# Two row groups moved to other places in TensorE's hand-written order of a Mamba and retrieval layer

## The chip, the cores and the metric

The kernel runs on one core of one Trainium2 chip. The metric is the device time of one execution in microseconds (us). The time before the change is 3161.11 us, the median of 3 runs (3151.85 to 3166.98).

## The reference

4096 tokens of 512 numbers pass through a Mamba-2 block and then through a retrieval layer, each followed by a residual and a layer norm, all in float32.

```
zxbcdt = u @ W_in                         # gate z, conv input xBC, step sizes dt
xBC = silu(causal_conv(xBC)); x, B, C = split(xBC)
y = scan over chunks of 64 with states    # 16 heads of 64
y = rms_norm((y + x*D) * silu(z)) @ W_out
x1 = layernorm(u + y)
h = silu(x1 @ W_up.T + b_up) @ W_down.T + b_down      # 256 wide
scores of h @ W_q.T against two sets of 64 keys, 8 heads, top 8 of 8x8 sums
64 picked rows of an embedding of 4096 (256 + 512 numbers each) per token:
out = sum over rows k of silu(h . down[k] * softmax[k]) * up[k]
result = layernorm(x1 + out)
```

## The kernel before

The tokens are cut into 32 tiles of 128. Tile `i` is in three stages at once: while the loop body `tile(i)` runs, the Mamba block of tile `i + 1` is computed (the calls under `if ahead`), tile `i` gets its projections up and down and its key scores, and the 64 picked rows of tile `i - 1` are worked off (the calls `old(...)`); the first four row groups of tile `i` itself close the body (`new(...)`). The picked rows have numbers 0 to 63.

**The rows.** POOL gathers row k of all 128 tokens with one indirect DMA (L276) into one of 13 ring buffers, k modulo 13. The gather of row k waits until row k - 13 has been used. For a row that VectorE (DVE) adds up, that is told row by row (`row_used`). For a row that TensorE (PE) adds up, it is told by the semaphore `row_pe`, which rises once at the end of each group with PE rows. DVE forms the dot product of each row with h (`dot`, L1129); ScalarE (ACT) makes the coefficients of a group (`coefs`, L645) and, for rows of PE, a diagonal matrix of them (`diag_c`, L654, four buffers); then PE multiplies diagonal and row in two passes (`weighted`, L500), or DVE adds the row two groups later (`weigh`, L1143).

The 64 rows are cut into 22 groups. Those that matter here, with P for a row of PE and D for one of DVE: group 13 holds rows 39 to 42 (PPPD), 14 rows 43 and 44 (PP), 15 rows 45 to 47 (PDD), 16 rows 48 to 51 (PPPP), 17 row 52 (D), 18 rows 53 to 55 (DDD), 19 rows 56 to 59 (PPPD), 20 row 60 (D), 21 rows 61 to 63 (PDD). So the gathers of rows 52 to 54 wait for group 13 on PE, those of rows 56 and 57 for group 14, that of row 58 for group 15, and those of rows 61 to 63 for group 16.

**The orders.** Each engine runs a list written out by hand, `tile` of its own block, and takes nothing out of turn. PE's order around the change: the turn of h (L481), key scores (L488), the two halves of the next tile's gate projection `z_proj` (L359, 8 passes each), group 13, the four masked sums `step_sums` (L368), `turn_x` (eight transposes of x, L376, then five small products up to L384, which raises `cb_mm`), groups 14 and 15, `y_off` (L396), group 16, `y_diag` (L412 and L415), groups 18 and 19, `state_in` (L425), `turn_y` (L431), group 21, `out_proj` (L441).

ACT's order there: 12 of the 16 masked steps (L700), coefs of group 13, `conv_silu` (L685), the last masked steps, the gates (L710, one for each half of `z_proj`), coefs of 14 and 15, the decays: four exponentials (L715, each after its masked sum), three small ones (L718 to L720, after `cb_mm`), a copy (L724); then `soft_exp`, `skip_term` (L691), coefs of 16 and 17 with a load of the activation table, and the first half of `end_decay` (L732).

DVE's order there: top 8 and their indices, groups 14 to 17 with sorting work between them, the indices of tile i (L1108), `scaled_x` (L982), `masked_products` (L991), groups 18 to 21, and then `scan_out` (L1000), `scan_add`, `scan_gate` (L1013). `scan_out` stands behind the dot product of row 63, and `turn_y` of PE waits for `scan_gate`.

Of the kernel before, what the change touches and what calls it, by code (L numbers as in the profile page):

```python
# [78 lines left out]
def build(nc, uT, u, W_in, W_out, W_upT, W_downT, W_q, keysT, embed, consts, iota8, conv_w, conv_b,  # L79
          dt_bias, A_log, D_cols, norm_cols, b_up, b_down, out):  # L80
    with ExitStack() as ctx:
# [206 lines left out]
        def _(pe):  # L288
# [40 lines left out]
            def xbc_proj(i, first, part):  # L329

                if part == 0:
                    pe.wait_ge(ut_in, 16 * i + 16)
                if part == 2:
                    pe.wait_ge(xr_ok, 3 * i + 1)
                elif not first:
                    pe.wait_ge(st_ok, 2 * i - 1 + part)
                lo, hi = part * BANK, min(part * BANK + BANK, CONV)
                for k in range(KD):
                    m = pe.matmul(bank[XR_BANKS[part]][:, 0:hi - lo], uT_v[:, k, :], w_in[:, k, DI + lo:DI + hi],  # L339
                                  start=(k == 0), stop=(k == KD - 1))  # L340
                m.then_inc(xr_mm, 1)

            def turn_xbc(i, first, part):

                pe.wait_ge(xr_ok, 3 * i + part + 1)
                if not first:
                    if part == 0:
                        pe.wait_ge(y_ok, 2 * i)
                    else:
                        pe.wait_ge(yT_ok, 2 * i)  # L350
                for c in range(4 * part, min(4 * part + 4, KC)):
                    m = pe.transpose(bank[XBC_BANKS[part]][:, (c % 4) * P:(c % 4 + 1) * P], seg[:, c, :], ident)
                m.then_inc(xbc_mm, 1)

            def z_proj(i, b):
                if b == 0:
                    pe.wait_ge(tap_ok, PARTS * (i + 1))
                for k in range(KD):
                    m = pe.matmul(bank[Z_BANKS[b]][:, :], uT_v[:, k, :], w_in[:, k, b * BANK:(b + 1) * BANK],  # L359
                                  start=(k == 0), stop=(k == KD - 1))  # L360
                m.then_inc(z_mm, 1)

            def step_sums(i, b):

                if b >= 2:
                    pe.wait_ge(z_ok, 2 * i + b - 1)
                pe.wait_ge(am_ok, 4 * i + b + 1)
                pe.matmul(bank[SEG_BANKS[b]][:, :], later, seg[:, 4 * b:4 * b + 4, :],  # L368
                          start=True, stop=True).then_inc(seg_mm, 1)

            def turn_x(i):
                pe.wait_ge(xc_ok, i + 1)
                for c in range(KX):
                    if c % 4 == 0:
                        pe.wait_ge(e_ok, 4 * i + 1 + c // 4)
                    m = pe.transpose(bank[XT_BANKS[c // 4]][:, (c % 4) * P:(c % 4 + 1) * P], xc[:, c, :], ident)  # L376
                    if c % 4 == 3:
                        m.then_inc(xT_mm, 1)
                pe.wait_ge(e_ok, 4 * i + 3)
                pe.transpose(bank[MISC][:, 0:P], xc[:, KX, :], ident)  # L380
                pe.matmul(bank[MISC][:, P:2 * P], xc[:, KX, :], xc[:, KX + 1, :], start=True, stop=True)
                pe.matmul(bank[MISC][:, 2 * P:2 * P + NH], upto, cur[:, 1, :], start=True, stop=True)
                pe.matmul(bank[MISC][:, 2 * P + NH:2 * P + 2 * NH], later, cur[:, 1, :], start=True, stop=True)
                pe.matmul(bank[MISC][:, 3 * P:3 * P + NH], ones, cur[:, 1, :], start=True, stop=True)\  # L384
                    .then_inc(cb_mm, 1)
# [60 lines left out]
            def turn_x1(i):  # L446
                pe.wait_ge(x1_ok, i + 1)
                for k in range(KD):
                    m = pe.transpose(bank[X1T][:, k * P:(k + 1) * P], x1_new[:, k * P:(k + 1) * P], ident)
                m.then_inc(x1T_mm, 1)  # L450

            def up_proj(i, b, first, ahead):
                if b == 0:
                    if first:
                        pe.wait_ge(w_up_in, 16)
                    pe.wait_ge(x1T_ok, i + 1)
                if b < 2:
                    pe.wait_ge(st_ok, 2 * i + b + 1)
                elif ahead:
                    pe.wait_ge(tap_ok, PARTS * (i + 1) + b - 1)  # L460
                for c in range(4 * b, 4 * b + 4):
                    for k in range(KD):
                        m = pe.matmul(bank[UP_BANKS[b]][:, (c % 4) * P:(c % 4 + 1) * P],  # L463
                                      w_up[:, k, c * P:(c + 1) * P], x1T[:, k, :], start=(k == 0), stop=(k == KD - 1))
                m.then_inc(h1_mm, 1)

            def down_proj(i, b, first, ahead):
                if b == 0:
                    if first:
                        pe.wait_ge(w_down_in, 16)  # L470
                pe.wait_ge(h1_ok, 4 * i + b + 1)
                for c in range(4 * b, 4 * b + 4):
                    m = pe.matmul(bank[DOWN][:, 0:DP], h1T[:, c, :], w_down[:, c, :],  # L473
                                  start=(c == 0), stop=(c == KU - 1))
                if b == 3:
                    m.then_inc(hp_mm, 1)
# [15 lines left out]
            def weighted(t, g, first):  # L492


                for k in rows_of(g, "P"):
                    n = PE_ROWS.index(k)
                    pe.wait_ge(diag_ok, len(PE_ROWS) * t + n + 1)
                    if n == 0 and not first:
                        pe.wait_ge(sum_ok, 3 * t - 2)
                    m = pe.matmul(bank[SUM][:, :], diag_c[:, (len(PE_ROWS) * t + n) % DIAGS, :], ring[:, k % RING, DP:ROW],  # L500
                                  start=(n == 0), stop=(n == len(PE_ROWS) - 1))
                if rows_of(g, "P"):
                    m.then_inc(row_pe, 1)

            def tile(i, first, ahead):

                def old(*which):
                    for g in which:
                        if not first:
                            weighted(i - 1, g, False)  # L510

                def new(*which):
                    for g in which:
                        weighted(i, g, first)

                if ahead:
                    xbc_proj(i + 1, False, 0)
                    xbc_proj(i + 1, False, 1)
                    xbc_proj(i + 1, False, 2)
                    turn_xbc(i + 1, False, 0)  # L520
                    turn_xbc(i + 1, False, 1)
                    turn_xbc(i + 1, False, 2)
                turn_x1(i)
                old(4, 5, 6)
                up_proj(i, 0, first, ahead)
                up_proj(i, 1, first, ahead)
                up_proj(i, 2, first, ahead)
                old(7, 8)
                up_proj(i, 3, first, ahead)
                down_proj(i, 0, first, ahead)  # L530
                old(9)
                down_proj(i, 1, first, ahead)
                old(10)
                down_proj(i, 2, first, ahead)
                down_proj(i, 3, first, ahead)
                turn_h(i, ahead)
                old(11, 12)
                key_scores(i, 0)
                key_scores(i, 1)
                if ahead:  # L540
                    z_proj(i + 1, 0)
                    z_proj(i + 1, 1)
                old(13)
                if ahead:
                    step_sums(i + 1, 0)
                    step_sums(i + 1, 1)
                    step_sums(i + 1, 2)
                    step_sums(i + 1, 3)
                    turn_x(i + 1)
                old(14, 15)  # L550
                if ahead:
                    y_off(i + 1, False)
                old(16, 17)
                if ahead:
                    y_diag(i + 1, False, 0)
                    y_diag(i + 1, False, 1)
                old(18, 19)
                if ahead:
                    state_in(i + 1)
                    turn_y(i + 1)  # L560
                old(20, 21)
                if ahead:
                    out_proj(i + 1, False, 0)
                new(0)
                if ahead:
                    out_proj(i + 1, False, 1)
                new(1, 2, 3)
# [777 lines left out]
```

## Time and profile before

| | |
|---|---|
| median of 3 runs | 3161.11 us |
| profiled execution | 3151.04 us, span 3149.2 us |
| granted TensorE clock, mean | 0.953 of full |
| PE busy | 2790.8 us, 89% |
| DVE busy | 2777.5 us, 88% |
| ACT busy | 2049.7 us, 65% |
| POOL busy | 2062.7 us, 65% |
| HBM read | 845.38 MB, mean 271 GB/s over the span |

All times are of one profiled execution, counted from its first instruction. A tile takes some 93 us. No engine is busy all the time; which one holds up the others has to be read from the waits. In a timeline a row gives start, duration, engine, line and operation, and in brackets the idle time ahead of it with what ended it.

### The profile page before, as it was taken

What the parts mean: (1) busy time and instruction counts of PE and PEld (TensorE: products, weight loads), DVE (VectorE), ACT (ScalarE), POOL (GpSimd) and SP (SyncE); (2) the same over time, 40 slices, a digit from 0 to 9 for tenths busy, and PEclk for the clock granted to TensorE, in tenths of its full rate; (3) what the DMA queues carried; (4) which work ended last, traced back from release to release, by engine and by line L of the source; (5) the groups of instructions that cost most, each with busy time, mean ns of one, the idle gap of its engine ahead of it and who ended that gap; (6) DMA issues with size and microseconds to landing.
All of it is one profiled execution on the core that took longest, in us unless ns stands there. A gap on an engine that the chain in (4) does not pass through costs nothing.

```text
span 3149.2 us, 44785 instructions
## 1 busy us (share of the span) xinstructions
PE 2790.8 (89%) x11776; PEld 1737.3 (55%) x11776; DVE 2777.5 (88%) x10160; ACT 2049.7 (65%) x6513; POOL 2062.7 (65%) x2056
## 2 busy tenths in 40 slices
PE   7989899998898999999899989899898999898863
PEld 4565456655555655555566545556555565555541
DVE  3489899998899999999899989999999999899986
ACT  3466766666776666676666676666676666677642
POOL 0066666676676667666667666666766666766676
PEclk9999999999999999999999999999999999999986
DMA  8088888888888888888888888888888888888888
GB/s 284 23 263 275 270 279 273 277 290 282 272 285 265 270 292 287 276 282 277 265 277 297 273 276 271 273 278 290 284 277 268 276 272 288 283 278 281 277 303 272
DMA packets 189855, 856.76 MB, mean 272 GB/s; under 512 B 36192, under 2 KB 39392, under 8 KB 189088
## 3 DMA queue, kind: packets, MB, share of 16 engines
q0 software_dynamic: 163840, 805.44, 77.0%
q1 hardware_dynamic: 19104, 34.87, 3.2%
q10 hardware_dynamic: 6656, 13.60, 1.2%
q8 instruction: 93, 1.52, 0.2%
q14 instruction: 162, 1.33, 0.1%
HBM read 845.38 MB, written 8.39 MB: 271 GB/s over the span
## 4 chain that ended last, share of the span: by engine, by line
PE 38%; DVE 32%; DMA 9%; POOL 9%; issue 7%; ACT 5%; POOLq 0%; SPq 0%; DVEq 0%; ACTq 0%
DVE bank L1143 14%; POOL ring L276 9%; DMA ring<-embed,idx 9%; PE bank L500 8%; DVE ring L1129 8%; PE bank L359 7%; DVE xc L974 6%; PE bank L339 5%; PE bank L441 4%; PE bank L488 4%; PE bank L368 3%; ACT xc L679 1%; PE bank L376 1%; PE bank L307 1%; ACT xskip L691 1%
## 5 line engine op out<-in xcount | busy, mean ns | idle before, releaser
L276 POOL DMA_INDIRECT ring<-embed,idx x2048 | 2061.4, 1007 | 1074.8 <-issue 532.3
L1143 DVE SCALAR_TENSOR_TENSOR bank<-ring,coef,bank 128x512 f32<-128x512 f32 x1312 | 992.4, 756 | 7.4 <-issue 0.2
L1129 DVE SCALAR_TENSOR_TENSOR ring<-ring,hcur 128x256 f32<-128x256 f32 x2048 | 823.8, 423 | 138.5 <-DMA ring<-embed,idx 136.1
L645 ACT ACTIVATE coef<-prob,zp 128x1 f32<-128x1 f32 x2048 | 456.0, 286 | 630.8 <-DVE ring L1129 625.4
L500 PE MATMUL bank<-ring,diag_c 128*128 128x512 f32 x1344 | 672.8, 631 | 115.9 <-ACT diag_c L654 101.3
L463 PE MATMUL bank<-zs,w_up 128*128 128x128 f32 x4096 | 502.2, 287 | 69.2 <-ACT zs L767 65.8
L463 PEld LDWEIGHTS bank<-zs,w_up 128*128 128x128 f32 x4096 | 496.2, 203 | 110.2 <-ACT zs L767 91.8
L500 PEld LDWEIGHTS bank<-ring,diag_c 128*128 128x128 f32 x1344 | 247.2, 199 | 379.2 <-issue 223.7
L974 DVE SCALAR_TENSOR_TENSOR xc<-raw,taps,xc 128x128 f32<-128x128 f32 x960 | 266.2, 351 | 102.6 <-ACT xc L679 102.5
L339 PE MATMUL bank<-w_in,ut 128*128 128x512 f32 (+1 forms) x768 | 285.8, 524 | 4.0 <-ACT seg L667 3.9
L654 ACT ACTIVATE diag_c<-cst,coef 128x128 f32<-128x128 f32 x672 | 234.8, 394 | 48.4 <-PE bank L500 38.0
L441 PE MATMUL bank<-w_out,xdec 128*128 128x512 f32 x512 | 245.5, 635 | 0.9 <-ACT xdec L749 0.9
L359 PE MATMUL bank<-w_in,ut 128*128 128x512 f32 x512 | 228.1, 599 | 4.4 <-ACT xc L679 4.4
L339 PEld LDWEIGHTS bank<-w_in,ut 128*128 128x128 f32 x768 | 143.9, 190 | 153.1 <-issue 124.6
L473 PE MATMUL bank<-w_down,seg 128*128 128x256 f32 x1024 | 226.3, 379 | 0.0
L773 ACT ACTIVATE seg<-bank,bup 128x128 f32<-128x128 f32 x512 | 145.4, 365 | 124.1 <-PE bank L463 124.1
L473 PEld LDWEIGHTS bank<-w_down,seg 128*128 128x128 f32 x1024 | 192.1, 190 | 24.8
L441 PEld LDWEIGHTS bank<-w_out,xdec 128*128 128x128 f32 x512 | 107.7, 212 | 149.8 <-issue 127.8
L1129 DVE DVE_READ_ACCUMULATOR ring<-ring,hcur 128x1 f32 x2048 | 177.0, 86 | 0.0
L359 PEld LDWEIGHTS bank<-w_in,ut 128*128 128x128 f32 x512 | 98.3, 192 | 128.5 <-issue 128.5
L700 ACT ACTIVATE seg<-cst,cur 128x128 f32<-128x128 f32 x512 | 155.6, 391 | 0.0
L415 PEld LDWEIGHTS bank<-xdt,seg 128*128 128x128 f32 x1024 | 133.6, 196 | 8.7 <-issue 8.7
(144 smaller groups left out, 3422.2 us busy)
## 6 DMA issues: line engine op xcount, KB each, us to landing
ring<-embed,idx POOLq DMA_INDIRECT x2048, 4.6
ring<-uT SPq DMA_DIRECT2D x4, 2048.0 KB, 14.2
ut<-uT SPq DMA_DIRECT2D x32, 256.0 KB, 6.5
zs<-u SPq DMA_DIRECT2D x32, 256.0 KB, 5.6
out<-acc SPq DMA_DIRECT2D x32, 256.0 KB, 4.6
w_up<-W_upT ACTq DMA_DIRECT2D x1, 4096.0 KB, 13.0
w_in<-W_in ACTq DMA_DIRECT2D x1, 2560.0 KB, 17.4
w_in<-W_in ACTq DMA_DIRECT2D x1, 2048.0 KB, 22.0
```

Of the source, the lines that this page charges most:

```text
L276: pool.indirect_dma_start(out=ring[:, k % RING, :], out_offset=None, in_=embed, in_offset=bass.IndirectOffsetOnAxis(ap=idx[:, half, k:k + ...
L339: m = pe.matmul(bank[XR_BANKS[part]][:, 0:hi - lo], uT_v[:, k, :], w_in[:, k, DI + lo:DI + hi], start=(k == 0), stop=(k == KD - 1))
L359: m = pe.matmul(bank[Z_BANKS[b]][:, :], uT_v[:, k, :], w_in[:, k, b * BANK:(b + 1) * BANK], start=(k == 0), stop=(k == KD - 1))
L441: m = pe.matmul(bank[OP][:, :], yT[:, c * P:(c + 1) * P], w_out[:, c, :], start=(c == 0), stop=(c == KX - 1))
L463: m = pe.matmul(bank[UP_BANKS[b]][:, (c % 4) * P:(c % 4 + 1) * P], w_up[:, k, c * P:(c + 1) * P], x1T[:, k, :], start=(k == 0), stop=(k == ...
L473: m = pe.matmul(bank[DOWN][:, 0:DP], h1T[:, c, :], w_down[:, c, :], start=(c == 0), stop=(c == KU - 1))
L500: m = pe.matmul(bank[SUM][:, :], diag_c[:, (len(PE_ROWS) * t + n) % DIAGS, :], ring[:, k % RING, DP:ROW], start=(n == 0), stop=(n == len(P ...
L645: m = act.activation(coef[:, k:k + 1], prob_v[:, k:k + 1], ACT.Silu, scale=zp[:, k:k + 1])
L654: act.activation(diag_c[:, (len(PE_ROWS) * t + n) % DIAGS, :], ident, ACT.Copy, scale=coef[:, k:k + 1]).then_inc(diag_ok, 1)
L974: m = dve.scalar_tensor_tensor(out=xc[:, c, :], in0=raw[:, c, j:j + P], scalar=taps[:, c, j:j + 1], in1=xc[:, c, :], op0=ALU.mult, op1=ALU ...
L1129: m = dve.scalar_tensor_tensor(out=ring[:, k % RING, 0:DP], in0=ring[:, k % RING, 0:DP], scalar=1.0, in1=hcur[:, :], op0=ALU.mult, op1=ALU ...
L1143: dve.scalar_tensor_tensor(out=total if n == len(DVE_ROWS) - 1 else running[:, :], in0=ring[:, k % RING, DP:ROW], scalar=coef[:, k:k + 1], ...
```

## The change

In PE's list, group 13 is put between the two halves of the next tile's gate projection, where it stood behind both, and group 14 between the four masked sums and `turn_x`, where it stood behind `turn_x`. Nothing else is touched: the orders of ACT, DVE and POOL and every semaphore's counts stay.

```diff
--- before.py
+++ after.py
@@ -539,15 +539,17 @@
                 key_scores(i, 1)
                 if ahead:
                     z_proj(i + 1, 0)
+                old(13)
+                if ahead:
                     z_proj(i + 1, 1)
-                old(13)
-                if ahead:
                     step_sums(i + 1, 0)
                     step_sums(i + 1, 1)
                     step_sums(i + 1, 2)
                     step_sums(i + 1, 3)
+                old(14)
+                if ahead:
                     turn_x(i + 1)
-                old(14, 15)
+                old(15)
                 if ahead:
                     y_off(i + 1, False)
                 old(16, 17)
```

## Rows read from the trace of the kernel before

**Rows 1.** Section 4 of the page: the chain that ended last, by engine.

```profile
PE 38%; DVE 32%; DMA 9%; POOL 9%; issue 7%; ACT 5%; POOLq 0%; SPq 0%; DVEq 0%; ACTq 0%
```

**Rows 2.** Waits of the whole span: total us, times, longest.

```profile
POOL ring L276 <- PE bank L500: 289.2, 151, 4.9
...
DVE ring L1129 <- DMA ring<-embed,idx: 136.1, 214, 2.5
...
ACT decay L718 <- PE bank L384: 24.0, 32, 1.2
```

**Rows 3.** Timeline of PE in tile 21, from 2100 to 2138 us.

```profile
2100.41 7.03 PE L359 MATMUL bank<-w_in,ut 128*128 128x512 f32 x16
2107.28 2.74 PE L500 MATMUL bank<-ring,diag_c 128*128 128x512 f32 x6
2109.86 3.60 PE L368 MATMUL bank<-seg,cst 128*128 128x512 f32 x8
2113.50 1.06 PE L376 MATMUL bank<-cst,xc 128*128 128x128 f32 x8
...
2115.37 2.82 PE L500 MATMUL bank<-ring,diag_c 128*128 128x512 f32 x6
...
2121.27 3.70 PE L500 MATMUL bank<-ring,diag_c 128*128 128x512 f32 x8 [1.36 <-ACT diag_c L654]
...
2136.32 1.54 PE L431 MATMUL bank<-cst,xdt 128*128 128x128 f32 x8 [2.93 <-DVE xdt L1013]
```

**Rows 4.** Timeline of ACT in the same tile.

```profile
2107.48 0.60 ACT L710 ACTIVATE zs<-bank 128x512 f32<-128x512 f32 x1 [2.71 <-PE bank L359]
...
2110.06 0.40 ACT L654 ACTIVATE diag_c<-cst,coef 128x128 f32<-128x128 f32 x1 [1.18 <-PE bank L500]
...
2115.55 0.19 ACT L718 ACTIVATE decay<-bank 128x16 f32<-128x16 f32 x1 [0.73 <-PE bank L384]
...
2120.81 1.28 ACT L654 ACTIVATE diag_c<-cst,coef 128x128 f32<-128x128 f32 x4
```

**Rows 5.** Timeline of POOL there: the gathers of rows 56, 60, 61 and 63.

```profile
2117.60 1.00 POOL L276 DMA_INDIRECT ring<-embed,idx  x1 [2.59 <-PE bank L500]
...
2122.67 2.08 POOL L276 DMA_INDIRECT ring<-embed,idx  x1 [0.30 <-issue]
2125.24 0.94 POOL L276 DMA_INDIRECT ring<-embed,idx  x1 [0.50 <-PE bank L500]
...
2127.77 0.94 POOL L276 DMA_INDIRECT ring<-embed,idx  x1 [0.30 <-issue]
```

**Rows 6.** Timeline of DVE there: the dot products of rows 60 and 63.

```profile
2127.97 0.43 DVE L1129 SCALAR_TENSOR_TENSOR ring<-ring,hcur 128x256 f32<-128x256 f32 x1 [0.96 <-DMA ring<-embed,idx]
...
2132.23 0.43 DVE L1129 SCALAR_TENSOR_TENSOR ring<-ring,hcur 128x256 f32<-128x256 f32 x1 [0.24 <-DMA ring<-embed,idx]
```

**Rows 7.** All 2048 gathers (line L276): from issue to landing.

```profile
DMA to landing us min/median/max: 3.8/4.6/8.6
```

**Rows 8.** Timeline of POOL in tile 15: the gather of row 61.

```profile
1563.48 1.04 POOL L276 DMA_INDIRECT ring<-embed,idx  x1 [0.30 <-issue]
```

**Rows 9.** Windows of 3.70 us over group 16 (L500): us, PE busy, clock, DMA share, GB/s.

```profile
248.40:252.10 3.70, 3.68 (x8) 1.00 0.86 294
...
1558.80:1562.50 3.70, 3.66 (x8) 1.00 0.56 202
...
2962.00:2965.70 3.70, 3.68 (x8) 1.00 0.89 297
```

**Rows 10.** Windows of 4.00 us from the start of turn_y (L431), same columns.

```profile
263.60:267.60 4.00, 1.97 (x8) 0.50 0.81 273
...
2977.00:2981.00 4.00, 1.96 (x8) 0.64 0.93 294
```

**Rows 11.** Windows from turn_y to out_proj's end, tiles 8 and 21 (PE, PEld, DVE, ACT, POOL busy; clock).

```profile
919.70:929.10 9.40, 9.09 (x26) 4.08 (x26) 8.46 (x28) 6.92 (x21) 7.27 (x8) 1.00 0.96 341
2136.30:2146.90 10.60, 10.58 (x27) 5.38 (x28) 9.35 (x28) 7.95 (x23) 8.01 (x9) 0.84 0.96 334
```

More of the change, by code:

```diff
@@ L541, in tile @@
                     z_proj(i + 1, 0)
-                    z_proj(i + 1, 1)
                 old(13)
                 if ahead:
+                    z_proj(i + 1, 1)
                     step_sums(i + 1, 0)
```

## The prediction

> **What bounds the kernel now.** I read the chain that ended last first. No engine owns it: PE has 38% of it, DVE 32%, DMA and POOL 9% each [rows 1]. So the tiles follow one another by a relay, and only a step on the relay is worth anything. The list of waits shows two places where this change can touch it: POOL stands 289.2 us in all waiting for PE to finish row groups, and DVE waits 136.1 us for gathered rows to land [rows 2].
>
> Then I followed one tile through the timelines of four engines, tile 21. PE runs without a gap through both halves of the gate projection, group 13, the masked sums, the turn of x and groups 14 and 15 (from 2100.41 on); then it sits idle for 1.36 us ahead of group 16, because ACT hasn't made its first diagonal, and for 2.93 us ahead of the turn of y, because DVE hasn't gated y [rows 3]. ACT's diagonals for group 16 begin at 2120.81, and the last wait ahead of them is at 2115.55: 0.73 us for the end of the turn of x [rows 4]. It is there in all 32 tiles, 24.0 us in total [rows 2]. POOL waits for group 14 before row 56 (2.59 us), and for group 16 before row 61 (0.50 us) [rows 5]. DVE waits 0.96 us for row 60 and 0.24 us for row 63, the last dot product ahead of the scan's output [rows 6]. So the relay is: turn of x on PE, decays, skip term and coefficients on ACT, group 16 on PE, gathers 61 to 63, dot product of row 63, scan on DVE, turn of y on PE. The wait for row 60, which comes from group 14, is the other, parallel strand. Both are nearly level: what one gives is lost where the other is late.
>
> **The change part by part.** Nothing is added or removed; 10 passes of PE in each of 30 tiles (`ahead` and old rows present) change places.
>
> *Group 13 forward.* Its 6 passes take 2.58 us (2107.28 to 2109.86 [rows 3]). They now run ahead of the second gate half. The diagonals are there by then: ACT makes them ahead of `conv_silu`, the last masked steps and the first gate, and has all of that behind it at 2104.77, when it begins to wait for the second half (2107.48 less 2.71 [rows 4]). POOL gets rows 52 to 54 free some 3.4 us sooner (one half of 6.87 us, 2100.41 to 2107.28). The second half of the projection ends 2.58 us later, and so does the gate that waits for it (2107.48 [rows 4]). Behind that gate on ACT stand the coefficients of 14 and 15 and the exponentials. ACT's 1.18 us wait for group 13 ahead of the diagonal at 2110.06 [rows 4] is gone, so it is 2.58 - 1.18 = 1.4 us late at the exponentials. Behind them comes the 0.73 us wait for the turn of x, so this alone would cost 0.7 us; but that wait moves too.
>
> *Group 14 forward.* Its 4 passes are two thirds of the 2.65 us or so that groups 14 and 15 take: 4 x 0.43 = 1.72 us (group 13's 2.58 over 6 gives 0.43 [rows 3]). The diagonals are ready: the second is now done at about 2111.8 and PE gets there at 2113.4. Group 14 ends 2.0 us sooner (the turn of x takes 1.87 us, 2113.50 to 2115.37), and POOL's wait of 2.59 us ahead of row 56 ends by as much sooner [rows 5]. That takes away DVE's 0.96 us at row 60 [rows 6]. The price is that the turn of x, and with it the signal that ACT awaits at 2115.55, comes 1.72 us later. This is more than the 0.7 us above and contains it. ACT has no further wait up to the diagonals at 2120.81, so they come 1.72 us later, and so does group 16: its idle time goes from 1.36 to 3.08 us. PE's own order in between (group 15, `y_off`) ends where it did.
>
> *What stands behind group 16.* The gathers of rows 61 to 63. Row 61 was issued 0.27 us after group 16's end (2121.27 + 3.70 = 2124.97, 2125.24 [rows 3, 5]), so it goes to 2126.96 and row 63 from 2127.77 to 2129.5. Row 63 landed by 4.46 us after its issue (2132.23 [rows 6]). With that, its dot product is 1.72 us late; with the shortest landing of any gather, 3.8 us [rows 7], it is 1.06 us late. POOL has paused longer, so the queue is emptier; I take the middle, 1.4 us. The 0.96 us won at row 60 can't be kept, because DVE then waits for 61 to 63. Everything after, scan, turn of y, output projection, next tile, follows the dot product of row 63. PE's later `y_diag` and `state_in` are covered: PE had 2.93 us idle there, and loses 1.72.
>
> In seven of 30 tiles POOL was late on its own account at row 61: the window over group 16 moved about 200 GB/s there instead of 290 [rows 9]. In tile 15 row 61 went out at 1563.48 [rows 8], 0.98 us after group 16's window closed, so 0.7 of the 1.72 us is swallowed; and row 63 wasn't waited for. I take 0.5 us (between 0 and 1.0). Sum of the order alone: 23 x 1.4 + 7 x 0.5 = 36 us; from 23 x 1.06 = 24 to 23 x 1.72 + 7 x 1.0 = 47.
>
> *The clock.* Ahead of the turn of y, PE is idle for about 3 us (2.93 in tile 21), and in the 4 us behind it the granted clock is 0.50 to 0.68 in 28 of 30 tiles, that is, much of it at 1.2 GHz in place of 2.4 [rows 10]. Behind the 1.36 us ahead of group 16 it is 1.00 in all 30 [rows 9]. The change makes these 1.36 into 3.08 us, which is the first kind. The price of such a stretch: from the turn of y to the output projection's end, tile 21 at clock 0.84 needs 10.5 us, tile 8 at 1.00 needs 9.25 [rows 11]: 1.25 us. As lost clock it is 10.6 x 0.16 = 1.7. Below it is nothing, if group 16 escapes. I take 1.25 us in 28 of 30 tiles, 35 us. It falls on group 16, hence on the gathers, and isn't hidden. Against it, the idle time ahead of the turn of y shrinks to about 2.7 us, and there some of the slow stretches may go: I take a quarter off, 9 us.
>
> The Trainium skill (TensorE: Matmul & The Clock Gate, Part 1: The HAM clock gate) says the array goes back to half clock when it has been idle and must be busy for a time before full clock returns; that speaks against this change. By that rule group 16 would run slowly and the time come out with this term, 3223 us; without the rule's effect at this place it would be 3197 us. The trace agrees behind the turn of y [rows 10], and shows no such effect after the shorter idle time ahead of group 16 [rows 9].
>
> Sum: 36 + 35 - 9 = +62 us. The profiled execution took 3151 us (span 3149.2), 10 below the median of the runs; on the median it gives 3161 + 62 = 3223 us.
>
> **The rivals.**
>
> *Order alone* (chance 0.27): group 16 keeps the full clock. +36 us, 3197 us (3185 to 3208). For it: the idle time is only just that of the turn of y. Against: 28 of 30 tiles there.
>
> *No difference* (0.09): the slow stretch leaves the turn of y and doesn't appear at group 16. Then -1.25 meets +1.4 per tile: +4 us, 3165 us. It needs an idle time ahead of the turn of y that no longer drops the clock; tile 8 shows that it can stay at 1.00 [rows 11].
>
> *Faster* (0.09): it does what the earlier gathers promise. If group 16 isn't held by the turn of x but by something that doesn't move, DVE saves 0.96 + 0.24 us a tile [rows 6] plus what lies behind it: some 1.3 x 30 = 39 us, 3122 us. It decides at ACT's L718: if that wait is not on the path to the diagonals of group 16, the gain stays; as soon as group 16 is late by over 0.3 us, row 63 takes it back. The 0.73 us idle there in front of a busy stretch up to 2120.81 [rows 4] speaks against it.
>
> *My forecast* (0.55): order and clock, 3223 us, own range 3200 to 3258 (the upper end 47 + 30 x 1.7 = +98).
>
> **How the numbers follow.** Range 3177 to 3258: from a little below the order term's lower bound to both terms at their upper ones; it leaves out the two last rivals. A difference below 0.5%, 16 us, can't be told from none in this kernel. Slower 0.82, same 0.09, faster 0.09.
>
> **What the profile after would show.** POOL's waits ahead of rows 52 and 56 shrink by 2 to 3 us each; the wait ahead of row 61 grows from 0.5 to 5 us or more. PE's idle time ahead of group 16 is about 3.1 us, ACT's L718 comes 1.7 us later relative to the turn of h. DVE no longer waits for row 60, but 1 to 3 us in all for rows 61 to 63. The clock over group 16 is below 1.00 in most tiles. Wrong would be: group 16 at its old distance from the turn of h, or gathers 61 to 63 landing before DVE asks for them.

## The result, and the profile after

The changed kernel takes 3228.91 us, the median of 4 runs (3225.9 to 3236.19), against 3159.94 us (3151.85 to 3166.98, 4 runs): a ratio of 1.0223 with a 95% interval of [1.0192, 1.0253] (the quotient of the two medians is 1.0218), 69 us slower. Ratios below are given in the same way, always to the kernel before on the same chip. The forecast was 3223 us. The profiled execution has a span of 3227.0 us, 77.8 more than before, at a mean granted clock of 0.942.

Where numbers below are given "in the middle tile", they are medians over tiles 2 to 30 of all the timelines, counted from the first instruction of DVE's block for the tile (`private`, L1047 before, L1049 after; behind L541 the lines of after are 2 higher). The mean distance from tile to tile went from 93.39 to 96.04 us, 2.65 more; 30 times that is 79.5.

The page after: busy time, and the chain that ended last by engine.

```profile
PE 2826.7 (88%) x11776; PEld 1759.8 (55%) x11776; DVE 2776.6 (86%) x10160; ACT 2041.1 (63%) x6513; POOL 2016.8 (62%) x2056
...
DVE 35%; PE 26%; POOL 13%; issue 12%; DMA 11%; ACT 3%; DVEq 0%; ACTq 0%; SPq 0%; POOLq 0%
```

PE's busy time is up by 35.9 us with the same instructions; the rows below show where it ran at the lower clock. In the chain POOL and DMA had 9% each [rows 1] and now have 13% and 11%: the gathers have become a larger part of the relay.

The waits of the whole span after: total us, times, longest.

```profile
POOL ring L276 <- PE bank L500: 331.9, 150, 6.9
DVE ring L1131 <- DMA ring<-embed,idx: 211.9, 239, 4.1
```

Both waits of [rows 2] grew, POOL's for the row groups from 289.2 us and DVE's for gathered rows from 136.1. PE in tile 21 after, the same stretch as [rows 3]:

```profile
2151.67 3.60 PE L359 MATMUL bank<-w_in,ut 128*128 128x512 f32 x8
2155.10 2.74 PE L500 MATMUL bank<-ring,diag_c 128*128 128x512 f32 x6
2157.68 3.60 PE L359 MATMUL bank<-w_in,ut 128*128 128x512 f32 x8
2161.11 3.60 PE L368 MATMUL bank<-seg,cst 128*128 128x512 f32 x8
2164.54 1.88 PE L500 MATMUL bank<-ring,diag_c 128*128 128x512 f32 x4
2166.26 1.04 PE L376 MATMUL bank<-cst,xc 128*128 128x128 f32 x8
...
2173.95 5.40 PE L500 MATMUL bank<-ring,diag_c 128*128 128x512 f32 x8 [3.08 <-ACT diag_c L656]
```

The new order is seen in the first six rows: group 13 between the gate's halves, group 14 between the masked sums (L368) and the transposes of x (L376). The last is group 16: 3.08 us of idle time ahead of it, and 5.40 us for the eight passes that took 3.70. ACT and then POOL of the same tile, to be read against [rows 4, 5]:

```profile
2168.24 0.18 ACT L720 ACTIVATE decay<-bank 128x16 f32<-128x16 f32 x1 [0.88 <-PE bank L384]
...
2173.50 1.28 ACT L656 ACTIVATE diag_c<-cst,coef 128x128 f32<-128x128 f32 x4
```

```profile
2166.70 0.94 POOL L276 DMA_INDIRECT ring<-embed,idx  x1 [3.50 <-PE bank L500]
...
2171.93 0.95 POOL L276 DMA_INDIRECT ring<-embed,idx  x1 [0.30 <-issue]
2179.62 0.94 POOL L276 DMA_INDIRECT ring<-embed,idx  x1 [6.74 <-PE bank L500]
```

ACT still has its one wait ahead of the diagonals, 0.88 us for the turn of x, and no other up to 2173.50. POOL's rows are the gathers of rows 56, 60 and 61. The wait ahead of row 61 is 6.74 us where it was 0.50. DVE at rows 61, 62 and 63 (compare [rows 6]):

```profile
2183.49 0.42 DVE L1131 SCALAR_TENSOR_TENSOR ring<-ring,hcur 128x256 f32<-128x256 f32 x1 [2.61 <-DMA ring<-embed,idx]
...
2185.42 0.43 DVE L1131 SCALAR_TENSOR_TENSOR ring<-ring,hcur 128x256 f32<-128x256 f32 x1 [0.83 <-DMA ring<-embed,idx]
...
2186.92 0.42 DVE L1131 SCALAR_TENSOR_TENSOR ring<-ring,hcur 128x256 f32<-128x256 f32 x1 [1.06 <-DMA ring<-embed,idx]
```

No wait for row 60 is left, and 4.50 us of waiting stand at the three rows behind it. The windows over group 16 after (us, PE busy, clock, DMA share, GB/s), against [rows 9]:

```profile
250.70:254.40 3.70, 3.65 (x8) 1.00 0.33 123
344.80:348.50 3.70, 3.70 (x5) 0.54 0.36 135
...
3038.40:3042.10 3.70, 3.70 (x5) 0.57 0.34 123
```

In 27 of 30 tiles the granted clock over group 16 is below 1.00 after; before it was in none. The DMA share there fell from 0.84 to 0.37 in the median of the 30 windows; POOL now stands still in that stretch (6.74 us ahead of row 61 in tile 21). Windows of 4 us from `turn_y`, against [rows 10]:

```profile
265.80:269.80 4.00, 1.29 (x8) 0.59 0.80 271
...
1227.50:1231.50 4.00, 1.05 (x8) 1.00 0.77 259
```

There hardly anything changed: full clock in 3 tiles where it was in 2.

The runs below came from five chips. On four of them the kernel before took 3622 to 3649 us in place of 3160, with 136 to 280 pieces of idle time on PE that have no releaser (169 to 323 us, where it is 3 us here); what causes this is not settled, so there only ratios within one chip are used, and the one experiment from a chip like the first (the kernel before 3156.03 us) carries most weight.

### The profile page after: what moved, and what is told of

It reads as the page before. It is cut to its first block, busy times and chain, and to the rows that moved or that the text cites. A ratio compares the mean times of both kernels' runs of the same rounds, so it can differ in the third digit from the quotient of the medians.

```text
span 3227.0 us, 44785 instructions
## 1 busy us (share of the span) xinstructions
PE 2826.7 (88%) x11776; PEld 1759.8 (55%) x11776; DVE 2776.6 (86%) x10160; ACT 2041.1 (63%) x6513; POOL 2016.8 (62%) x2056
## 4 chain that ended last, share of the span: by engine, by line
DVE 35%; PE 26%; POOL 13%; issue 12%; DMA 11%; ACT 3%; DVEq 0%; ACTq 0%; SPq 0%; POOLq 0%
POOL ring L276 13%; DVE bank L1145 12%; DMA ring<-embed,idx 10%; DVE ring L1131 8%; DVE xc L976 5%; PE bank L500 5%; PE bank L339 4%; PE bank L359 4%; PE bank L441 3%; PE bank L488 2%; PE bank L368 2%; ACT xc L681 1%; DVE i L1061 1%; PE bank L307 1%; DVE v L1055 1%
## 5 line engine op out<-in xcount | busy, mean ns | idle before, releaser
L276 POOL DMA_INDIRECT ring<-embed,idx x2048 | 2015.5, 984 | 1198.0 <-issue 532.4
L1131 DVE SCALAR_TENSOR_TENSOR ring<-ring,hcur 128x256 f32<-128x256 f32 x2048 | 813.1, 418 | 213.9 <-DMA ring<-embed,idx 211.9
L500 PE MATMUL bank<-ring,diag_c 128*128 128x512 f32 x1344 | 724.0, 668 | 167.2 <-ACT diag_c L656 152.2
L463 PE MATMUL bank<-zs,w_up 128*128 128x128 f32 x4096 | 508.7, 289 | 69.2 <-ACT zs L769 65.8
L500 PEld LDWEIGHTS bank<-ring,diag_c 128*128 128x128 f32 x1344 | 264.8, 213 | 458.8 <-issue 243.8
L441 PE MATMUL bank<-w_out,xdec 128*128 128x512 f32 x512 | 237.3, 617 | 1.2 <-ACT xdec L751 1.2
L1131 DVE DVE_READ_ACCUMULATOR ring<-ring,hcur 128x1 f32 x2048 | 166.4, 81 | 0.0
L712 ACT ACTIVATE zs<-bank 128x512 f32<-128x512 f32 x64 | 37.5, 586 | 168.5 <-PE bank L359 168.5
```

The costliest lines, as they stand in the source:

```text
L276: pool.indirect_dma_start(out=ring[:, k % RING, :], out_offset=None, in_=embed, in_offset=bass.IndirectOffsetOnAxis(ap=idx[:, half, k:k + ...
L441: m = pe.matmul(bank[OP][:, :], yT[:, c * P:(c + 1) * P], w_out[:, c, :], start=(c == 0), stop=(c == KX - 1))
L1131: m = dve.scalar_tensor_tensor(out=ring[:, k % RING, 0:DP], in0=ring[:, k % RING, 0:DP], scalar=1.0, in1=hcur[:, :], op0=ALU.mult, op1=ALU ...
```

## The experiments

### One move at a time

The change has two halves. `e1` is the kernel before with group 13 between the gate's halves and nothing else; `e2` with group 14 ahead of `turn_x` and nothing else. `e12` is `e2` once more on another chip.

The edit of `e1` against the kernel before:

```diff
                     z_proj(i + 1, 0)
+                old(13)
+                if ahead:
                     z_proj(i + 1, 1)
-                old(13)
-                if ahead:
```

The edit of `e2` and `e12` against the kernel before:

```diff
                     step_sums(i + 1, 3)
+                old(14)
+                if ahead:
                     turn_x(i + 1)
-                old(14, 15)
+                old(15)
```

> Only group 13 is moved. My theory (the turn of x releases ACT, ACT releases group 16, group 16 releases the gathers of rows 61 to 63): ACT's exponentials come 1.3 us later, which eats the 0.73 us wait at L718, so group 16 starts 0.5 to 0.7 us later, its idle time goes to about 2 us, and the clock falls there in some tiles. Period of a tile +0.4 to +1.2 us, in all 3172 to 3197 us. Rival (the two moves share the loss evenly): about 3195 us. Rival (this half is harmless): 3160 us, group 16 at its old distance.

Measured: 3641.3 us against 3642.29, ratio 0.9993 [0.9963, 1.0022]. PE in one tile of it:

```profile
1896.93 1.06 PE L376 MATMUL bank<-cst,xc 128*128 128x128 f32 x8 [1.34 <-ACT seg L715]
...
1904.70 3.70 PE L500 MATMUL bank<-ring,diag_c 128*128 128x512 f32 x8 [1.37 <-ACT diag_c L654]
```

ACT is late at the exponentials, but PE takes that up ahead of the transposes: their first write goes to the bank that ACT's first exponential has to read before, and PE waits 1.34 us for that. So PE's list moves back together with ACT's. ACT's wait for the turn of x stays at 0.73 us, and the idle time ahead of group 16 at 1.37 us, at full clock in all 30 tiles. The 2 us that I had expected there are wrong. Against a run of the kernel before on a chip of this kind (`e9`), the turn of x ends 1.1 us later in the middle tile (22.93 against 21.82 us behind `private`), and group 16 starts 0.6 us later (28.68 against 28.09). The second number is smaller because in `e9` ACT takes up the decays 0.56 us after the turn of x has ended, and in `e1` 0.04 us after it; that it is near the 0.7 of the prediction is chance. The runs show no loss. Group 13 is harmless on these chips.

> Only group 14 is moved. My theory: the turn of x ends 1.4 us later as it does with both moves, so group 16 starts 1.4 us later, with 3.1 us of idle time ahead of it and the half clock behind it; nearly the whole loss, 3215 to 3230 us. Rival (even shares): about 3195 us. Rival (the earlier gathers 56 to 60 outweigh it where group 13 isn't moved): 3140 to 3160 us.

Measured: 3765.35 us, ratio 1.033 [1.0263, 1.0398]. The idle time ahead of group 16 is 3.9 us in the middle tile, and group 16 takes 5.8 us and is slow in all 30 tiles.

> Group 14 alone moved, once more. Theory: on a chip where the kernel before takes 3160 us, group 16 starts 1.4 us later with 3.1 us of idle time (not the 3.9 us of the first set, where ACT was itself held up), half clock over it: ratio 1.018 to 1.026, nearly the whole loss. Rival (both moves share it): 1.010 to 1.015.

Measured: 3778.85 us against 3648.86, ratio 1.0358 [1.0298, 1.0419]. Group 16, and the wait for gathered rows over the span:

```profile
2645.37 5.74 PE L500 MATMUL bank<-ring,diag_c 128*128 128x512 f32 x8 [3.92 <-ACT diag_c L656]
```

```profile
DVE ring L1131 <- DMA ring<-embed,idx: 376.4, 256, 5.1
```

So on these chips group 14 alone brings the loss and group 13 alone doesn't. The loss is even larger than that of both moves together (1.0123, `e5` below), and `e2` and `e12` agree on it. But it isn't a clean price of group 14. The idle time is 3.92 us here and 3.08 in `e5`, because ACT ends its skip term 1.4 to 1.6 us later, counted from `private`, after the same end of the turn of x (23.28 us in all three). The delay sits at ACT's first decay:

```profile
2639.66 0.18 ACT L720 ACTIVATE decay<-bank 128x16 f32<-128x16 f32 x1 [3.99 <-remote]
```

It starts 1.9 to 2.0 us after PE's last pass of the turn of x has ended, where that is 0.04 us in the median tile of before, after, `e1`, `e5` and `e10`, and the profile finds no sender for the signal that ended the wait ("remote"). What causes it is open. This half never ran on a chip where the kernel before takes 3160 us.

### The whole change again, on a chip of the other kind

> The changed kernel once more, beside the kernel before on the same chip, so that the other runs of this set can be held against it. Theory and rivals: a ratio of 1.02 on a chip where the kernel before takes 3160 us. On a chip where it takes 3640 us, the first two sets of kernels there say 1.02 to 1.035 if group 16's lateness and its half clock are the cause (group 14 alone gave 1.033 there), and 1.00 to 1.01 if the further idle time of that chip hides them.

Measured: 3687.84 us against 3649.12, ratio 1.0123 [1.0054, 1.0192]. The idle time ahead of group 16 is 3.08 us again, and it is slow in 22 of 30 tiles (mean 5.13 us). The sign and the mechanism stay; the ratio is about half as far from 1, in a kernel whose tiles also wait for other things.

### Order without the clock

`e3` and `e10` fill the idle time: after, with the second product of `y_off` computed four times in place of once (the same values into the same place, the last one counts), which gives PE 2.6 us of work ahead of group 16 and moves nothing that ACT or POOL wait for.

```diff
-                for b in range(2):
+                for b in (0, 1, 1, 1, 1):
```

> The changed kernel, with the second product of y_off computed four times in place of once (2.6 us of PE work in the 3.1 us of idle time ahead of group 16, same values). My theory (1.7 us of the loss per tile are the half clock over group 16): the clock over group 16 is 1.00, it ends 1.7 us sooner, and 28 x 1.5 or so = 40 to 50 us come back: 3180 to 3190 us. Rival (the clock costs nothing on the path, the lateness of group 16 alone counts double): 3225 to 3232 us. Rival (the half clock only goes elsewhere): above 3210 us with a clock below 1.00 behind another wait.

Measured: 3663.05 us against 3642.29, ratio 1.0068 [1.0038, 1.0099]. Idle time ahead of group 16 0.5 us, slow in no tile.

> The changed kernel with the second product of y_off computed four times, once more, in the hope of a chip where the kernel before takes 3160 us; there the two terms can be parted. My theory (of the 2.6 us a tile, 1.7 are the half clock over group 16 and some 1.2 the lateness of the turn of x): group 16 in 3.7 us at clock 1.00, 3175 to 3190 us, ratio 1.005 to 1.010. Rival (the clock is not on the path): ratio 1.018 or more. Where the kernel before takes 3640 us: 1.005 to 1.009 as in the first set, against 1.012 for the changed kernel.

Measured, on a chip where the kernel before takes 3156.03 us: 3190.83 us (3180.71 to 3192.93), ratio 1.01 [1.0069, 1.0131]. PE in one tile of it:

```profile
2140.40 4.46 PE L396 MATMUL bank<-state,xc 128*128 128x512 f32 x10
2145.36 3.70 PE L500 MATMUL bank<-ring,diag_c 128*128 128x512 f32 x8 [0.51 <-ACT diag_c L656]
```

Its windows over group 16 (us, PE busy, clock, DMA share, GB/s):

```profile
251.50:255.20 3.70, 3.69 (x8) 1.00 0.42 125
...
2145.40:2149.10 3.70, 3.66 (x8) 1.00 0.34 126
...
2999.80:3003.50 3.70, 3.69 (x8) 1.00 0.37 123
```

Group 16 starts 27.32 us behind `private` in the middle tile, in this kernel and in after alike, so it comes as late in both. What differs is what PE did ahead of it: it worked in place of standing still, and the clock is 1.00 in all 30 tiles. This splits the result in two:

| middle tile, us | before | filled (`e10`) | after |
|---|---|---|---|
| group 16 starts | 25.91 | 27.32 | 27.32 |
| group 16 ends | 29.61 | 31.02 | 32.72 |
| gather of row 61 issued | 29.88 | 31.30 | 32.99 |
| dot product of row 63 | 37.06 | 38.45 | 39.96 |
| mean from tile to tile | 93.39 | 94.59 | 96.04 |

The order alone costs 34.8 us (3190.83 less 3156.03; by the interval 22 to 41), and the clock over group 16 the rest of the 69, some 36 us (1.0223 x 3156 = 3226, less 3191). After and `e10` come from different sets of runs; the two intervals together leave some 25 to 53 us for the clock. The stretch from 24 to 40 us behind `private` holds the difference: the time in it times the share of the clock that was not granted adds up, over 30 tiles, to 0 us before, 49.5 after and 0 in `e10`. In the 45 us behind it the same sum is 92, 89 and 73 us.

The execution of after alone says the same, since three of its tiles kept the full clock over group 16. From the start of group 16 to the dot product of row 63 it takes 11.26 us in the mean in these three and 12.84 in the other 27, and to the next tile's `private` 66.96 and 68.71: the lower clock there is passed on, 1.6 to 1.8 us each time.

### Group 16 kept from being late

The other way to undo the mechanism is to shorten ACT's path. In `e4` and `e11` ACT makes the coefficients and diagonals of group 16 ahead of the skip term (2.44 us in the timeline after) and those of group 17 behind it; PE's order is that of after. `e7` is the same edit in the kernel before.

```diff
+                old(16)
                 if ahead:
                     skip_term(i + 1)
-                old(16, 17)
+                old(17)
```

> The changed kernel, with the coefficients of group 16 ahead of the skip term in ACT's list (2.4 us sooner). My theory (ACT's late diagonals are the only thing that spoils the change): group 16 starts about 24.9 us after h is made, with under 1 us of idle time, at full clock; the gathers 61 to 63 go out 4.5 us sooner than in the changed kernel, and DVE waits for none of rows 60 to 63: the scan 1 to 1.4 us sooner than before the change, 3110 to 3140 us. Rival (PE's own list or the masked products bound it then): same as before the change, 3150 to 3165 us. Rival (the cause is not ACT): 3220 to 3230 us.

Measured: 3593.89 us against 3642.29, ratio 0.9897 [0.9838, 0.9956]; idle time ahead of group 16 0.8 us, slow in 2 tiles.

> The changed kernel with ACT's coefficients of group 16 ahead of the skip term, once more, in the hope of a chip like that of the last run. Theory: group 16 starts 24.5 to 25.5 us after h is made, idle time under 1 us at clock 1.00, rows 61 to 63 go out before DVE asks for them; the scan is 0.5 to 1.4 us sooner than in the kernel before: ratio 0.985 to 0.995. Rival (another wait takes the gain): 0.995 to 1.005. Where the kernel before takes 3640 us: 0.99 as in the first set.

Measured: 3570.19 us against 3648.86, ratio 0.9783 [0.9754, 0.9811]. Group 16 in one tile:

```profile
2501.80 3.70 PE L500 MATMUL bank<-ring,diag_c 128*128 128x512 f32 x8 [0.77 <-issue]
```

Slow in no tile. With group 16 no longer behind the skip term the two moves cost nothing that shows: this version beats the kernel before on both chips where it ran. The changed kernel didn't run on these two; on the third chip of the kind its ratio is 1.0123. Nor did this version run where the kernel before takes 3160 us, so what it would do there is open.

> The kernel before, with the coefficients of group 16 ahead of the skip term in ACT's list, PE's order as before. My theory: the 1.36 us of idle time ahead of group 16 go, group 16 ends 1.3 us sooner; but row 56 still waits for group 14 behind the turn of x, POOL is held by row 60, and so only 0.2 to 0.7 us a tile come of it: ratio 0.993 to 0.998. With the moves (the run with both) it should be clearly more. Rival (ACT's order alone is worth all of it): ratio 0.985 to 0.990, the same as with both.

Measured: 3701.06 us against 3649.12, ratio 1.0149 [1.0078, 1.0221]: slower, where I had expected a gain. Group 16 has no idle time ahead of it and takes 3.6 us. POOL's gather of row 59, which holds up that of row 60, and DVE's wait for row 60:

```profile
2587.86 2.83 POOL L276 DMA_INDIRECT ring<-embed,idx  x1 [0.30 <-issue]
```

```profile
2595.82 0.42 DVE L1130 SCALAR_TENSOR_TENSOR ring<-ring,hcur 128x256 f32<-128x256 f32 x1 [1.76 <-DMA ring<-embed,idx]
```

The other strand, group 14 to row 60, stayed where it was, and holds DVE now: the gather of row 59 is issued beside DVE's product of the masks and takes 2.83 us in place of 0.94, so that of row 60 starts at 2590.99. That explains why nothing was won; it doesn't explain a loss of 1.5%. The idle time without a releaser on PE is 323 us in this run, more than in any other; the cause of the loss is open. Side by side `e4`, `e11` and `e7` still say that the edit on ACT pays with the new order and not with the old, on these chips.

### The clock without the order

`e6` is the kernel before with seven copies of one element on ACT behind the skip term, so that group 16's diagonals come later and nothing on PE changes place (the lines that declare `pad` and `pad_ok` are left out below).

```diff
                     skip_term(i + 1)
+                if ahead and not first:
+                    act.wait_ge(pad_ok, i - 1)
+                    for n in range(7):
+                        m = act.activation(pad[:, n, :], ident[:, 0:1], ACT.Copy)
+                    m.then_inc(pad_ok, 1)
                 old(16, 17)
```

> The kernel before, nothing moved on PE, with seven one-element copies into a spare buffer on ACT behind the skip term (about 1.3 us), so that the diagonals of group 16 come as late as in the changed kernel. My theory (the lateness of group 16 is the whole loss): idle time ahead of group 16 2.7 us, clock below 1.00 there, as slow as the changed kernel or a little slower, since row 56 is not earlier: ratio 1.015 to 1.025. Rival (the moves themselves cost, through the gate's lateness or the earlier gathers): ratio 1.000 to 1.005.

Measured: 3665.22 us against 3649.12, ratio 1.0028 [0.999, 1.0066]: not told from none. The idle time ahead of group 16 is 2.5 us, and the window's clock is below 1.00 in 10 of 30 tiles (us, PE busy, clock, DMA share, GB/s):

```profile
270.10:273.80 3.70, 3.70 (x6) 0.60 0.67 209
375.70:379.40 3.70, 3.65 (x8) 1.00 0.72 244
```

This is a weak test. The idle time falls short of the 3.1 us of after; group 16 starts only 0.75 us later than in `e9`, the kernel before on a chip of this kind; and without the delay 9 tiles (`e9`) or 7 (`e8`) are slow there already, so one to three were added. That no loss is seen speaks neither for the mechanism nor against it. What the run adds is a point between 1.4 and 3.1 us of idle time: a third of the tiles fall, and two thirds don't.

> The kernel before once more, one look, for its trace beside those of the runs above. Theory: if it takes some 3640 us, its trace shows idle time of PE that nothing in the program releases, inside the up projection and of several us a tile, which the 3160 us trace lacks, while ahead of group 16 stand the same 1.36 us at full clock. If it takes 3160 us, this is another chip than in the two sets above.

Measured: one run, 3640.89 us, beside 3621.67. Group 16 in one tile:

```profile
1897.91 5.40 PE L500 MATMUL bank<-ring,diag_c 128*128 128x512 f32 x8 [1.88 <-issue]
```

I had expected 1.36 us and full clock everywhere. On this chip the unchanged kernel has 1.88 us there and is slow in 9 of 30 tiles. That is part of why the ratios on such chips are smaller: the kernel before already pays the clock's price in a third of its tiles.

### The stretch behind the turn of y

`e8` asks whether the slow stretch at `turn_y`, of which I had taken a quarter off, is worth anything: the kernel before, with the second product of `state_in` computed four times (the same values again), to fill PE's idle time ahead of `turn_y`. That is 5.8 us on a chip of this kind (`e9`, middle tile), not 3, and 2.7 us of it are left.

```diff
-                    pe.matmul(bank[ST_BANKS[b]][:, :], btok, xdec[:, b * BANK:(b + 1) * BANK],
-                              start=True, stop=True).then_inc(st_mm, 1)
+                    for _ in range(4 if b else 1):
+                        m = pe.matmul(bank[ST_BANKS[b]][:, :], btok, xdec[:, b * BANK:(b + 1) * BANK],
+                                      start=True, stop=True)
+                    m.then_inc(st_mm, 1)
```

> The kernel before, with the second product of state_in computed four times in place of once (2.6 us of PE work in the 3.1 us of idle time ahead of the turn of y, same values). My theory of the clock's price: the clock over the turn of y and the output projection is 1.00, 1.2 us a tile come back, ratio 0.985 to 0.993. Rival (the stretch there is covered by ACT's work on the state): 0.997 to 1.003. Rival (the fill makes PE late itself): above 1.003.

Measured: 3645.5 us, ratio 0.9989 [0.9954, 1.0024]. Windows from `turn_y` in it:

```profile
940.10:944.10 4.00, 1.97 (x8) 0.50 0.85 265
...
3232.20:3236.20 4.00, 1.06 (x8) 1.00 0.98 300
```

The clock there is 1.00 in 16 of 30 tiles, against 3 in `e9`, and no time is won. By itself that is weak: 13 tiles at the prediction's 1.25 us would be 16 us, a ratio of 0.9955, and the interval just takes that in. The trace of `e10` is clearer. In 8 of its tiles the 4 us behind the start of `turn_y` have the full clock, in 22 not. The output projection ends 9.28 us behind that start in the mean of the 8 and 10.62 us in that of the 22, but the next tile's `private` comes 51.66 and 51.71 us behind it. So a slow stretch at this place isn't passed on to the next tile, while one over group 16 is: what hangs on group 16 are three gathers that DVE waits for.

## Why the prediction was right

Its likeliest case, order and clock, is what happened, 5.9 us from the forecast. By its own steps:

**Group 13 forward.** POOL's wait ahead of row 52, 3.35 us in tile 21 before, is gone, and the gather goes out 3.05 us sooner (14.93 to 11.88 us in the middle tile; 3.4 was said). ACT ends its exponentials 1.27 us later in after (1.4 was said). The 0.7 us that this move alone was to cost at group 16 left out a wait: the transposes of x wait for ACT's first exponential, which has to read their bank before. In `e1` that makes the turn of x 1.1 us late; it isn't swallowed by ACT's 0.73 us of waiting. In after it doesn't show, because group 14 stands ahead of the transposes: in tile 21 the first exponential ends at 2165.89, and they begin at 2166.26.

**Group 14 forward.** The gather of row 56 goes out 2.2 us sooner (22.24 to 20.07) and DVE's wait for row 60 is gone, as said. But POOL's wait ahead of row 56 didn't shrink: it is 3.50 us against 2.59 [rows 5], because POOL comes to it 3 us sooner, too. A wait's length is a difference of two times and is a poor sign when both ends move. L720 comes 21.60 us behind `private` in tile 21 in place of 20.19, and group 16 starts 1.41 us later; 1.72 was worked out. The difference is a small gain on PE that I had left out: `turn_x` starts 1.49 us later in the middle tile (18.14 to 19.63), though 1.72 us of passes were put ahead of it, so some 0.2 us less is lost between the masked sums and the transposes when row passes stand between them; it ends 1.42 us later. The idle time still came out at the 3.08 us forecast, since `y_off` ended 0.29 us sooner: 1.36 + 1.41 + 0.29.

**Rows 61 to 63.** The wait ahead of row 61 grew to 6.74 us, and DVE waits 4.50 us in all at the three rows, above the 1 to 3 I gave. Most of the surplus is the slow group 16: `e10`, which has the order without it, waits 2.46 us at the same place in the tile shown above. And of these 2.46 some 1.1 are no loss: DVE comes to the rows sooner, since the wait for row 60 is gone (its dot product starts 31.56 us behind `private` in the middle tile, 32.67 before). The dot product of row 63, on which the rest hangs, is 1.39 us late by the order (`e10`); 1.4 was taken.

**The seven tiles with a late POOL.** I gave them 0.5 us each by the order and the others 1.4. To treat them apart was right, and the gap is larger. The mean distance between the two `private` around the dot product of row 63, us:

| | before | filled (`e10`) | after |
|---|---|---|---|
| the 23 other tiles | 92.83 | 94.60 | 95.90 |
| the seven tiles | 95.27 | 94.99 | 96.21 |

By the order the 23 lose 1.77 us each, and the seven win 0.28, because they were 2.4 us longer before the change. Their POOL wasn't simply late on its own account: it is in exactly these seven that the gather of row 59 is issued beside DVE's product of the masks (L991, 2.29 us) and takes 2.64 to 3.03 us, which makes rows 60 to 63 late. In tile 15:

```profile
1558.93 2.88 POOL L276 DMA_INDIRECT ring<-embed,idx  x1 [0.30 <-issue]
```

In the other 23 it is the gather of row 60 that takes longer, 1.89 to 2.37 us (2.08 in tile 21, from 2122.67 [rows 5], beside the product from 2121.63). In after the gathers of rows 56 to 60 are out ahead of the product in 28 tiles (row 60 at 2171.93 with 0.95 us, the product at 2172.91). So the change took a delay away that only seven tiles paid for. By these means the order's sum is 23 x 1.77 - 7 x 0.28 = 39 us, against my 36 = 23 x 1.4 + 7 x 0.5; by the runs it is 34.8. Both stand inside the 24 to 47 of the prediction, with one term too small and the other too large.

The Trainium skill (GPSIMD Engine Reference, 1. Specifications) lists GpSimd's SBUF interfaces as shared with VectorE, with contention from DVE instructions that have two SBUF inputs; L991 is one, and the row of 2.08 us agrees with it, as do the others: of the kernel before's 2048 gathers 31 took over 1.5 us to issue, and every one of them began during L991.

**The clock.** 1.25 us in 28 of 30 tiles, 35 us, were forecast. Group 16 is slow in 27 tiles, 5.40 us in place of 3.70 in most, 1.57 us more in the mean; from tile to tile 1.45 us come through (94.59 to 96.04), which is 43 us over 30 tiles, and by the medians of the runs some 36 us in all. That the 35 are met so closely is in part luck: the 1.25 us were read from the stretch behind the turn of y, at the end of the output projection, where a slow clock isn't passed on to the next tile.

The rule of the Trainium skill (TensorE: Matmul & The Clock Gate, Part 1: The HAM clock gate) that the prediction set beside this term holds here in its direction: `e10` against after shows that standing still ahead of group 16 is what makes it slow.

**The 9 us taken off.** This step failed. The idle time ahead of `turn_y` went from 3.08 to 2.97 us in the middle tile, not to 2.7, and the slow stretches stayed (full clock in 3 tiles, 2 before). It was also wrong in kind: such a stretch is not passed on to the next tile (51.66 and 51.71 us in `e10`), and `e8`, which freed 13 of them, won nothing. Without it the sum is 36 + 35 = 71, and 3161 + 71 = 3232 us; measured were 3228.91.

**The rivals.** *Order alone* describes `e10` (3190.83 us against its 3197), and after isn't it. *No difference* needed `turn_y` to be spared and group 16 to keep its clock; neither happened. *Faster* was to be decided at L718: if that wait isn't on the path to group 16's diagonals, the gain stays. `e11` takes group 16 off that path by an edit, and the kernel is then 2.2% faster than before on its chip. That fits a gain of the earlier gathers which only this path takes back, but how much of the 2.2% is the two moves and how much the edit is not split cleanly, since `e7`, the edit alone, lost time for reasons left open.

## What to carry to other kernels

Before putting work forward in one engine's list, look at what signal it is put in front of: 1.7 us of group 14 ahead of the turn of x went through ACT, group 16 and three gathers and reached the scan almost whole, and freeing ring buffers 2 to 3 us sooner didn't make up for it. Such a delay can be charged twice, as lateness and as a lower clock on the matmuls behind the longer idle time; filling that idle time with repeated work tells the two apart in one run. And before a slow stretch gets a price, ask who waits behind it: the same clock costs some 1.5 us a tile over group 16 and nothing that shows behind the turn of y.

## What the runs showed of the hardware

**Idle time ahead of group 16 and the granted clock behind it.** Fourteen profiled executions, each with the same eight passes there (30 tiles; slow means over 4.1 us for them, or in `e6` a clock below 1.00 in the window):

| idle time ahead in the middle tile, us | slow tiles of 30 |
|---|---|
| 0.0 to 0.8 (`e7`, `e3`, `e10`, `e11`) | 0 in each |
| 0.8 (`e4`) | 2, both where the idle time was 1.6 |
| 1.4 (before, `e1`) | 0 in each |
| 1.9 (`e8`, `e9`) | 7, 9 |
| 2.5 (`e6`) | 10 |
| 3.1 (after, `e5`) | 27, 22 |
| 3.9 (`e2`, `e12`) | 30, 29 |

I had taken the clock for kept or lost at a place, as before shows it. It is a share of the tiles that grows with the idle time, and some fall behind idle times much shorter than the 3 us of [rows 10]. The points at 0.0, 0.8, 1.6, 1.9, 2.5 and 3.9 us come only from the chips of the other kind, where PE stands idle at other places too; on those like the first there are 0.5, 1.4 and 3.1 us, with 0, 0 and 27 slow tiles. The slow form of this group is 5.40 us most often, against 3.70, 1.7 us more; behind 3.9 us of idle time it is 5.8 to 5.9.

**A gather's issue beside a long DVE product.** A gather that POOL begins during L991 (128x2048 float32, both inputs in SBUF) waits that product out: in the kernel before all 31 gathers with an issue over 1.5 us began 0.08 to 1.29 us behind the product's start, and ended 0.81 to 0.82 us behind its end. The 24 others that overlap it began before it or at most 0.04 us into it, and took the usual 0.94 to 0.95 us.

**Two kinds of chip.** The same kernel took about 3160 us where the first result and `e10` were taken and 3622 to 3649 us on four other chips, 15% more, with idle time that the profile gives to no releaser: on PE 169 to 323 us there, 3 us here, on ACT 185 to 266 against 12, on DVE 127 to 202 against 3.5. Waits whose signal has no sender in the profile add 571 to 792 us over all engines there and none here. It looks as if the engines' instructions or signals come late; that is argued from these rows alone and wasn't tried. Each of these chips was used for one set of runs, so whether the chip or its state at that hour makes the kind isn't told. Ratios of small changes don't carry over between the two kinds: after is 1.0223 on the one and 1.0123 on the other.
